# A deformable-convolution stage on one core: sampling in five matmuls per tile in place of six, with VectorE making seven of nine products of hats

## The reference

```
out = relu(group_norm(conv1x1(x, w1)))                  # 1024 -> 256 channels
om = conv3x3(out, w_off) + b_off                         # 27 channels: 9 x-offsets, 9 y-offsets, 9 masks
py, px = grid_y + ky + off_y, grid_x + kx + off_x        # for each of 9 taps and 196 pixels
sampled = bilinear_sample(out, py, px) * sigmoid(mask)   # zero outside the picture
out = relu(group_norm(einsum('bckhw,ock->bohw', sampled, w2)))
out = group_norm(conv1x1(out, w3))                       # 256 -> 1024 channels
return relu(out + x)
```

## Time and profile before

| what | value |
|---|---|
| median of three runs | 2961.8 us |
| profiled execution, its own time | 2961.04 us |
| its span | 2958.8 us |
| TensorE busy | 2908.3 us (98%) |
| VectorE busy | 2366.0 us (80%) |
| ScalarE busy | 1795.0 us (61%) |
| GpSimd busy | 455.3 us (15%) |
| granted TensorE clock, mean | 0.994 |
| sampling matmuls | 3840 |
| masking on GpSimd, first and last start | 944.3 and 2852.4 us |

### The profile page before, as it was taken

One profiled execution on the slowest core, in us unless ns is written; L12 is line 12 of the kernel. 1 busy time (PEld: TensorE's weight loads), 2 busy tenths in 40 slices (PEclk: granted clock), 3 DMA queues, 4 the chain that ended last, 5 costly groups with the idle time before them and its releaser, 6 DMA issues.

```text
span 2958.8 us, 46593 instructions
## 1 busy us (share of the span) xinstructions
PE 2908.3 (98%) x16518; PEld 2865.9 (97%) x16518; DVE 2366.0 (80%) x5000; ACT 1795.0 (61%) x3281; POOL 455.3 (15%) x305
## 2 busy tenths in 40 slices
PE   9999999999998999999999999999999999999997
PEld 9999999999997899999999999999999999999997
DVE  5655889865666688888888888888888888888885
ACT  4544332346665466767666676676766767667664
POOL 0000000000000122221222212222122221222210
PEclk9999999999999899999999999999999999999998
DMA  7774111035663344444444444444544444444431
GB/s 270 215 238 134 44 44 40 10 124 218 245 232 130 122 136 152 156 150 158 150 153 154 148 159 151 153 155 150 158 150 156 152 149 159 148 152 156 149 121 74
DMA packets 209208, 437.39 MB, mean 148 GB/s; under 512 B 18640, under 2 KB 170192, under 8 KB 203344
## 3 DMA queue, kind: packets, MB, share of 16 engines
q1 hardware_dynamic: 159408, 326.82, 32.7%
q10 hardware_dynamic: 49568, 107.60, 11.8%
HBM read 307.71 MB, written 126.64 MB: 147 GB/s over the span
## 4 chain that ended last, share of the span: by engine, by line
PE 63%; DVE 3%; DMA 1%; ACT 1%; SPq 0%; issue 0%; POOL 0%; ACTq 0%; DVEq 0%; POOLq 0%
PE sample L87 7%; PE deform L87 7%; PE sample L88 7%; PE sample L92 7%; PE deform L92 7%; PE deform L88 6%; PE work L87 6%; PE work L92 6%; PE work L88 6%; PE work L74 1%; PE work L76 1%; PE work L75 1%; DMA hats<-hat_scratch 1%; PE work L2046 1%; DVE x L1715 1%; DVE s_lo L1819 1%
## 5 line engine op out<-in xcount | busy, mean ns | idle before, releaser
L1465 ACT ACTIVATE v_hi<-sample 128x392 fp32r<-128x392 f32 (+1 forms) x640 | 291.7, 463 | 315.1 <-PE sample L92 306.0
L87 PE MATMUL sample<-s_hi,aT_hi 98*128 98x392 f32 (+1 forms) x1280 | 417.5, 331 | 8.9 <-DVE v_lo L1827 8.9
L1675 POOL TENSOR_TENSOR hats<-hats 98x784 f32<-98x784 f32 x160 | 341.0, 2131 | 523.1 <-DMA hats<-hat_scratch 504.3
L88 PE MATMUL sample<-s_hi,aT_lo 98*128 98x392 f32 (+1 forms) x1280 | 413.3, 328 | 0.0
L87 PE MATMUL deform<-v_hi,w_w 128*128 128x392 f32 x1152 | 403.5, 350 | 0.0
L88 PE MATMUL deform<-v_hi,w_w 128*128 128x392 f32 x1152 | 393.1, 341 | 0.0
L1827 DVE TENSOR_TENSOR v_lo<-sample,v_hi 128x392 fp32r<-128x392 f32 (+1 forms) x640 | 326.9, 518 | 66.5 <-ACT v_hi L1465 62.2
L92 PE MATMUL sample<-s_lo,aT_hi 98*128 98x392 f32 (+1 forms) x1280 | 315.1, 327 | 0.0
L92 PE MATMUL deform<-v_lo,w_w 128*128 128x392 f32 x1152 | 310.4, 342 | 0.0
L1456 ACT ACTIVATE s_hi<-hats 98x784 fp32r<-98x784 f32 x288 | 245.4, 852 | 98.5 <-DVE x L1715 71.7
L1819 DVE TENSOR_TENSOR s_lo<-hats,s_hi 98x784 fp32r<-98x784 f32 x288 | 281.1, 976 | 2.4 <-ACT s_hi L1456 1.4
(11 more groups left out here) (227 smaller groups left out, 7282.9 us busy)
## 6 DMA issues: line engine op xcount, KB each, us to landing
hats<-hat_scratch SPq DMA_DIRECT2D x768, 150.1 KB
x<-in_x SPq DMA_DIRECT2D x64, 784.0 KB, 5.8
in_home<-y_scratch ACTq DMA_DIRECT2D x248, 196.0 KB, 3.3
out<-x ACTq DMA_DIRECT2D x62, 784.0 KB, 4.4
y_home<-in_x SPq DMA_DIRECT2D x32, 784.0 KB, 5.0
y_scratch<-y_out SPq DMA_DIRECT2D x16, 1568.0 KB, 5.9
terms<-in_x SPq DMA_DIRECT2D x30, 784.0 KB, 4.7
y_scratch<-y_home SPq DMA_DIRECT2D x15, 1568.0 KB, 5.1
```

Source lines behind the costliest of these rows:

```text
L87: nc.tensor.matmul(out, w_hi, x_hi, start=start, stop=False)
L88: nc.tensor.matmul(out, w_lo, x_hi, start=False, stop=False)
L1465: nc.scalar.activation(v_hi[:, group % 2, c, 0:taps_of(g), i, :], sample[:, t % 2, 0:cols(g)].rearrange("p (k s) -> p k s", s=PIX), ACT.Co ...
L1675: nc.gpsimd.tensor_tensor(hats[:, slot, 0:2, 0:n], hats[:, slot, 0:2, 0:n], hats[:, slot, 2:3, 0:n].broadcast_to([HALF, 2, n]), ALU.mult). ...
```

## The change

The 196 input pixels are cut into 126 (9 rows of the picture, `A_ROWS`) and 70 (5 rows, `R_ROWS`). A tile's product then has these parts: the first 126 need three matmuls. Of the rest's three parts, hi x hi (70 partitions) shares one matmul with 56 partitions of lo x hi, and hi x lo (70) shares one with the other 14 of lo x hi: 126 and 84 partitions. That makes five matmuls. For this

- aT has four planes: high and low of the first 126, and twice the high of the rest with parts of its low beneath, which `copy_aT`, two new DMAs on SyncE's queue per image, moves there within SBUF;
- the second y-hats block is loaded with 4 of its 5 rows again beneath, so a unit's load is four pieces of 126, 70, 56 and 126 partitions where it was three of 98;
- `copy_s`, a new DMA on SyncE's queue for each unit, moves 14 partitions of s_hi beneath s_lo after `rest_s`;
- the last matmul of both tiles of a unit is issued after the second tile's fourth, once that copy has landed, and only these free the tiles for `part_v`.

GpSimd makes products 6 and 7 only; VectorE makes 0 to 5 and 8, product 0 in the step before under the name `fresh`. A group norm's two small reductions become one. `rest_aT` becomes two subtractions. The order of every list is changed. Three semaphores of layer 0 are used on.

```
+UPPER = 9
+LOWER = SIDE - UPPER
+A_ROWS = UPPER * SIDE
+R_ROWS = LOWER * SIDE
+TWICE = A_ROWS - R_ROWS
+C_ROWS = R_ROWS + R_ROWS - TWICE
 GROUPS = 5
 UNITS = 2 * GROUPS - 1
 TILES = 4 * GROUPS
 OFFCH = 27
 SPREAD_ROWS = 96
-BY_POOL = (0, 1, 2, 6, 7)
+BY_POOL = (6, 7)
...
-        nc.vector.tensor_reduce(self.sums[:, 0, :], parts[:, :, :, 1], AX_X, ALU.add).then_inc(self.done, 1)
         dve.wait_ge(self.done, base + self.SUMMED_M2)
-        nc.vector.tensor_reduce(self.sums[:, 1, :], self.square[:], AX_X, ALU.add).then_inc(self.done, 1)
+        nc.vector.tensor_reduce(self.sums[:], parts[:, :, :, 1:3].rearrange("p i t m -> p m i t"), AX_X,
+                                ALU.add).then_inc(self.done, 1)
...
+        aT = sb("aT", [A_ROWS, 2, 4, CMID], F32R)
...
+        aT_rest = a_f[0:R_ROWS, :, :, 0:P].bitcast(F32R)
...
+                parts = [(i, slice(0, n))]
                 if u == UNITS - 1:
+                    parts = [(i, slice(i * PIX, (i + 1) * PIX)) for i in range(2)]
+                for i, at in parts:
+                    n = at.stop - at.start
+                    y_hat, x_hat = (hats_at[p.n % 2, e, i, :, t0:t0 + n] for e in range(2))
+                    for dst, rows in ((hats[:, slot, 0, at], slice(0, UPPER)), (hats[0:R_ROWS, slot, 1, at], slice(UPPER, SIDE)),
+                                      (hats[R_ROWS:A_ROWS, slot, 1, at], slice(UPPER, SIDE - 1))):
+                        sp.dma_start(dst, y_hat[rows].unsqueeze(1).broadcast_to([rows.stop - rows.start, SIDE, n])
                                      ).then_inc(hats_loaded[slot], 16)
+                    sp.dma_start(hats[:, slot, 2, at], x_hat.unsqueeze(0).broadcast_to([UPPER, SIDE, n])
                                  ).then_inc(hats_loaded[slot], 16)
...
+            @of_pair
+            def copy_s(p, u):
+                unit = UNITS * p.n + u
+                sp.wait_ge(s_lo_made, unit + 1)
+                sp.dma_start(s_lo[R_ROWS:C_ROWS, unit % 2, 1].bitcast(F32), s_hi[TWICE:R_ROWS, unit % 2, 1].bitcast(F32)
+                             ).then_inc(s_moved[unit % 2], 16)
+            @of_pair
+            def copy_aT(p, i):
+                sp.wait_ge(aT_lo_made, 2 * p.n + i + 1)
+                if i == 1:
+                    sp.wait_ge(aT_moved, aT_moved_before + 64 * p.n + 32)
+                for plane, rows in ((2, slice(0, TWICE)), (3, slice(TWICE, R_ROWS))):
+                    n = rows.stop - rows.start
+                    sp.dma_start(aT[R_ROWS:R_ROWS + n, i, plane].rearrange("p (k c) -> p k c", k=KM).bitcast(F32),
+                                 aT_rest[rows, :, i].bitcast(F32)
+                                 ).then_inc(aT_moved, 16)
...
-                at_least(act, transposed, 2 * p.n)
+                if p.n:
+                    act.wait_ge(aT_moved, aT_moved_before + 64 * p.n)
                 nc.scalar.activation(a_f.rearrange("p k i s -> p k (i s)"), work[:, 0:2, 0:PAIR],
                                      ACT.Copy).then_inc(a_raw, 1)
...
+                nc.scalar.activation(aT[:, i, 0], work[0:A_ROWS, 2 * i, 0:CMID], ACT.Copy)
+                nc.scalar.activation(aT[0:R_ROWS, i, 2:4],
+                                     work[0:R_ROWS, 2 * i, CMID:2 * CMID].unsqueeze(1).broadcast_to([R_ROWS, 2, CMID]),
                                      ACT.Copy).then_inc(aT_hi_made, 1)
...
-                make_s(now, 0)
-                make_s(now, 1)
-                make_s(now, 2)
...
-                nc.vector.tensor_tensor(aT_lo[:, i].rearrange("p h c -> p (h c)"), work[0:HALF, 2 * i, :],
-                                        aT_hi[:, i].rearrange("p h c -> p (h c)").bitcast(F32),
+                nc.vector.tensor_tensor(aT[:, i, 1], work[0:A_ROWS, 2 * i, 0:CMID], aT[:, i, 0].bitcast(F32),
+                                        ALU.subtract)
+                rest = work[0:R_ROWS, 2 * i, CMID:2 * CMID].rearrange("p (k c) -> p k c", k=KM)
+                nc.vector.tensor_tensor(aT_rest[:, :, i], rest,
+                                        aT[0:R_ROWS, i, 2].rearrange("p (k c) -> p k c", k=KM).bitcast(F32),
                                         ALU.subtract).then_inc(aT_lo_made, 1)
...
+                if (u - 1) % UNITS in BY_POOL:
                     dve.wait_ge(s_made, unit)
...
                     for k in range(KM):
-                        last = nc.tensor.transpose(work[0:HALF, 2 * i, (h * KM + k) * P:(h * KM + k + 1) * P],
-                                                   a_f[:, k, i, h * HALF:(h + 1) * HALF], ident[:])
+                        last = nc.tensor.transpose(work[0:at.stop - at.start, 2 * i, (h * KM + k) * P:(h * KM + k + 1) * P],
+                                                   a_f[:, k, i, at], ident[:])
...
-                for h in range(2):
-                    products_of_high(nc, sample[:, t % 2, 0:n], aT_hi[:, i, h, c * P:(c + 1) * P],
-                                     aT_lo[:, i, h, c * P:(c + 1) * P], s_hi[:, unit % 2, h, at:at + n], start=(h == 0))
+                to, a_part = sample[:, t % 2, 0:n], aT[:, i, :, c * P:(c + 1) * P]
+                high, low = s_hi[:, unit % 2, :, at:at + n], s_lo[:, unit % 2, :, at:at + n]
+                nc.tensor.matmul(to, a_part[:, 0], high[:, 0], start=True, stop=False)
+                nc.tensor.matmul(to, a_part[:, 1], high[:, 0], start=False, stop=False)
+                if t in (0, 2):
+                    pe.wait_ge(aT_moved, aT_moved_before + 64 * p.n + 32 * (i + 1))
+                nc.tensor.matmul(to, a_part[:, 2], high[:, 1], start=False, stop=False)
                 if c == 0:
                     pe.wait_ge(s_lo_made, unit + 1)
-                for h in range(2):
-                    last = product_of_low(nc, sample[:, t % 2, 0:n], aT_hi[:, i, h, c * P:(c + 1) * P],
-                                          s_lo[:, unit % 2, h, at:at + n], stop=(h == 1))
-                last.then_inc(sampled, 1)
+                nc.tensor.matmul(to, a_part[:, 0], low[:, 0], start=False, stop=False)
+                if c == 0:
+                    return
+                pe.wait_ge(s_moved[unit % 2], s_moved_before[unit % 2] + 16 * (unit // 2 + 1))
+                for c in range(2):
+                    nc.tensor.matmul(sample[:, c, 0:n], aT[0:C_ROWS, i, 3, c * P:(c + 1) * P], low[0:C_ROWS, 1],
+                                     start=False, stop=True).then_inc(sampled, 1)
```

337 lines of the change are left out of this document (170 added, 167 removed).

## The result

The changed kernel takes 3078.0 us (median of 4 runs, 3067.9 to 3090.4), the kernel before 2961.8. The ratio is 1.040, 95% interval 1.037 to 1.042: slower, where 2874 us was forecast. That is 50 us beyond rival B (3028), the slowest case named. The kind is B's, a wait of TensorE for the copy of s_lo, but the place is one copy per pair of images, not nine. The profiled execution has a span of 3084.1 us and takes 3085.9.

A forecast was written before the change was run, and what follows sets the result against it. TensorE was taken to bound the kernel, before and after. 2961 us less 106 for the matmuls saved, plus 19 for waits at sample_tile(17), b_lo and unit 6, gave 2874, range 2850 to 2914.

The forecast's parts named there:

- rival B: TensorE waits at the end of each of nine units for the copy of s_lo: 3028 us, chance 0.08.
- Part 1: TensorE's sampling: a sixth of the matmuls goes, saving 3.30 us per pair, 106 us in all.
- the floor: TensorE's period per pair if all of the matmul saving stays on the path: 58.25 us, or 2855 in all.
- Part 2: VectorE: three more products cost 2.64 us per pair, fewer hold-ups by GpSimd give back 2.5; 54.0 of 58.25 us busy.
- Part 3: SP's queue: 41 of 58 us used; a copy takes 0.5 to issue and 2.5 to land; unit 6 is tight.
- Part 5: Unit 0's product on VectorE ahead of sample_tile(17): no slack, 0.3 us of wait expected there per pair.
- rival A: Hats late, VectorE's queue stands: make_s(0) waits 1.5 to 2 us, or make_s(3) waits too; 2925 us, chance 0.18.
- the lag of the load: Unit 0's hats, last issue to landing: 3.66 us before, plus 0.8 taken for the larger load.
- The uneven pieces: Hats loads by the skill's rule: busiest engine carries 56 partitions for 42, load grows 1.2 us for 0.8, 13 us more.
- Part 4: Joined last matmuls of a unit's two tiles cost nothing; b_lo at conv3 has no slack left.

The follow-up runs named there:

- e13: Changed kernel with VectorE's products 8, 0 and 3 later, unit 0's copy of s_lo ahead of load_hats(3), and no fourth piece of hats after three units: 2890.6 us.
- e7: Kernel before the change, with only products 0, 1 and 2 moved to VectorE: 2958.0 us, ratio 0.9997.
- e8: Changed kernel in its own order, without the fourth piece of hats loads after the first three units (result wrong): 2892.9 us.
- e5: Changed kernel with VectorE's products 8, 0 and 3 later and unit 0's copy of s_lo issued ahead of load_hats(3): 2913.4 us.
- e14: Changed kernel with unit 0's copy of s_lo issued by ScalarE and VectorE's products 8, 0 and 3 later: 2901.3 us.
- e16: Changed kernel with unit 0's copy of s_lo held back on SyncE's queue until rest_s of unit 1 is done: 3122.8 us.
- e11: Changed kernel with the fourth piece of hats cut from 56 partitions to 14 from the fourth unit on (result wrong): 2973.3 us.
- e9: Changed kernel with unit 0's copy of s_lo issued by ScalarE in place of SyncE: 3049.5 us.
- e1: Changed kernel with unit 0's copy of s_lo issued ahead of load_hats(3) on SyncE's queue: 3135.9 us.
- e6: Changed kernel with VectorE's products 8, 0 and 3 later, unit 0's copy of s_lo still behind load_hats(3): 3010.7 us.

## Why the prediction was wrong

**Part 1, right.** 3200 sampling matmuls, still 0.18 apart. The spacings of all sampling matmuls sum to 20.0 us a pair before and to 16.8 in e13, where hardly a wait is left: 3.2 for the forecast 3.30. e13's period is (2782.3 - 943.1) / 31 = 59.33 against the floor of 58.25; 0.62 of the difference are waits listed in the trace, and what the other 0.46 are stays open.

**Part 2, right in its sum, wrong in one place.** e7 prices the move of the three products at nothing. In the changed kernel the additions of y and x take 621 and 416 ns in the mean, as forecast. But the possibility named there, that a remaining product of GpSimd's comes beside other work in the new order, came about at rest_a: 976 ns before at each of its 32 runs, now 2007 at the median. GpSimd's product of unit 6 lies beside it, here from 1972.45 to 1974.34:

```profile
1972.45 1.89 POOL L1716 TENSOR_TENSOR hats<-hats 126x784 f32<-126x784 f32 x1 [4.14 <-DMA hats<-hat_scratch]
1973.17 2.00 DVE L1805 TENSOR_TENSOR x_lo<-in_home,x_hi 128x784 fp32r<-128x784 f32 x1 [0.18 <-ACT x_hi L1456]
...
1975.23 0.42 PE L79 MATMUL work<-x_hi,wob_w 128*96 128x392 f32 x1 [0.32 <-DVE x_lo L1805]
```

That costs VectorE 0.8 us a pair in the mean, and TensorE 13.3 us in all. It meets the product in 21 of the 32 pairs (over 1.2 us); in e8, with the lighter loads, in 18, in e5 and e14 in one.

**Part 3, the step that failed first.** Two statements of it were wrong. Issue and landing of the copy were taken as 0.5 + 2.5 = 3.0 us, as if nothing were ahead of it. For a copy alone that is more than enough (2.13 to 2.15 for units 2, 6 and 7), but behind load_hats(3) they are 6.26 at the median up to TensorE's start, and 4.66 with that load older (e16). And the cover was laid out for units 2 to 6 and 8, but not for unit 0, whose copy stands behind aT's two copies and the load of unit 3: 4.0 us from the end of rest_s(0) to the issue, most of which the text's own "a copy can stand behind a load being issued, 3.1 us" would have given. Of the 6.26, SyncE's issue is 0.84, where 0.5 was taken. With 3.0 the copy would have been there 0.7 to 1.0 us ahead of its use (2.24 us of wait in the period shown, 2.60 in the mean, against an excess of 3.3). With the 4.0 us of queue gone, a landing of 6.26 would have been in time as well. So by these numbers each of the two errors alone would have left hardly a wait; together they leave 2.60 us a pair. The eight other copies leave no wait of TensorE: their cover holds. Rival B had priced a late landing of 5 us, but spread it over nine units.

**Part 5 and rival A.** The wait at make_s(0) was forecast at 0.3; TensorE waits 0.63 at sample_tile(17), VectorE 1.05 at product 0. The term that was mis-sized is the lag of the load, 5.2 in the period shown for the forecast 4.46. By the semaphore's records the load of unit 0 landed 3.55 us after its last issue's end before and 5.08 now (medians over 24 pairs). So it grew by 1.5 us, where 0.8 was taken. Rival A named make_s(3) as well, and it is the dearest: 2.60 us of VectorE's time a pair, passed on by its queue. Product 8, at 1.7, was not considered; TensorE pays for it at sample_tile(13), 1.05. Both A and B happened, and in the text they were alternatives.

**The uneven pieces.** By the Trainium skill, "DMA: Bandwidth & Descriptors", section "Why a DMA increments its semaphore by 16 and not by 1", uneven pieces would load the busiest engine more and the sum was 2887. The forecast said that no row shows single engines. The trace's records of the loads' semaphores agree with that rule: one load has 24 updates before (three pieces of 7 rows), 31 in the changed kernel (9, 5, 4 and 9 rows), 26 in e8 (9, 5 and 9), 41 in e11, whose small piece is 14 partitions of one row, and a copy of 14 partitions has 15. Each count is the sum of the rows, or of the 14 partitions, and one more for each piece. By that rule the busiest engines carry 56 partitions in the changed kernel, 42 before and in e8 and 43 in e11, so e8 and e11 take bytes away and even the spread out at once. No run here changes the spread alone, and its share of the 185 us is open. The 13 us that the forecast's estimate by it added were far too few in any case.

**Part 4.** The joined matmuls cost nothing beside the copy, as forecast. The wait forecast at conv3(0) for b_lo is not among TensorE's dearest.

**The half clock, a term that was missing.** Around the end of 16 of the 24 waits for the copy the granted clock falls to its lower level, and matmuls start 0.33 apart. At the other 8 it stays at 1.00, though their waits are no shorter (2.1 to 4.0 us). That is the 3.13 us a pair of above, and an estimated 1.4 us of time, a quarter on top of the 5.0 of waits. In e5, e13 and e14 the granted clock is 1.00 over the whole of these 24 periods.

**The sum.** Over the middle 24 periods: 58.25 floor + 5.0 waits + 1.4 half clock = 64.65 of the 65.8 measured there; where the other 1.1 lie stays open. The causes do not add: taking away the copy's wait alone is worth 29 us (e9) or less than nothing (e1), VectorE's waits alone 67 (e6), both 165 to 177 (e5, e14). That both causes act is shown by these. Of the copy's 6.2 us, 2.1 are its own and 4.1 come with the load ahead of it. For the loads of hats themselves no run parts transport from waiting behind others: e8 and e11 give the price of lighter loads, not a model of it.

## What to carry to other kernels

When a step becomes dependent on a DMA, lay out every instance of it in the issuing queue, the first of a period above all, with what is issued ahead of it, and take its landing from transfers that have others ahead of them. Where an engine that works in order has little idle time left, put an instruction that waits for a load behind the ones that the bounding engine needs next. Price rivals that can happen together as one case too, and change a queue's order only together with the order of the engine that it feeds.
